# A decoder layer on one core: score shift on GpSimd, value sums in PSUM, scan factor in k's bank, tokens added by an accumulating DMA

## The reference

```python
x = x + rwkv(layernorm(x))          # time mix with a scan over tokens, then its own ffn
x = x + xattn(layernorm(x), ctx, ctx)
x = x + ffn(layernorm(x), U1, V1, b1, U2, V2, b2)

# in rwkv: h = ln1(x); xk, xv, xr = mixes of h and the h of the token before
k, v, sr = xk @ Wk.T, xv @ Wv.T, sigmoid(xr @ Wr.T)
y, (aa, bb, pp) = scan over tokens:  y = (e1*aa + e2*v) / (e1*bb + e2), with running maximum pp
x = x + (sr * y) @ Wo.T
h = ln2(x); kk = square(relu(xk @ Wkey.T)); x = x + sigmoid(xr @ Wrec.T) * (kk @ Wval.T)

# xattn: inside each token, 16 heads of 16; head i attends to heads 0..i of the same token's ctx
scores = einsum('bsqd,bskd->bsqk', qh, kh) / 4 ; masked below the diagonal; softmax
out    = einsum('bsqk,bskd->bsqd', attn, vh)

# ffn: low rank, 256 -> 64 -> 1024 -> gelu -> 64 -> 256
```

## Time and profile before

| | |
|---|---|
| Median of 3 runs | 1250.37 us (1248.64 to 1262.07) |
| Time of the profiled execution | 1249.77 us |
| Its span, first to last instruction | 1247.8 us |
| Mean granted TensorE clock | 0.945 |
| Busy: PE, DVE, ACT, POOL | 83%, 89%, 75%, 69% of the span |
| HBM | 29.38 MB read, 8.39 MB written |

### The profile page before, as it was taken

One profiled execution on the slowest core, in us unless ns is written; L12 is line 12 of the kernel. 1 busy time (PEld: TensorE's weight loads), 2 busy tenths in 40 slices (PEclk: granted clock), 3 DMA queues, 4 the chain that ended last, 5 costly groups with the idle time before them and its releaser, 6 DMA issues.

```text
span 1247.8 us, 14567 instructions
## 1 busy us (share of the span) xinstructions
PE 1032.6 (83%) x3584; PEld 584.6 (47%) x3584; DVE 1111.0 (89%) x2172; ACT 935.8 (75%) x2005; POOL 867.1 (69%) x783
## 2 busy tenths in 40 slices
PE   2679598989898989989798989989698998869515
PEld 1336263636455463736355463736346363626202
DVE  3755999999999999999999999999999999988681
ACT  4877779698888889796788879697688979464413
POOL 0112968788795968687595968688496968777680
PEclk9789799999999999999899999999899999979657
DMA  5010101001010101010010102001010101010000
GB/s 186 17 51 18 34 1 34 18 18 51 17 51 18 51 17 50 0 48 20 17 50 18 51 0 68 0 18 50 17 50 17 34 1 51 1 34 18 1 17 17
DMA packets 38964, 38.39 MB, mean 31 GB/s; under 512 B 2932, under 2 KB 38648, under 8 KB 38904
## 3 DMA queue, kind: packets, MB, share of 16 engines
q1 hardware_dynamic: 38904, 37.77, 9.5%
HBM read 29.38 MB, written 8.39 MB: 30 GB/s over the span
## 4 chain that ended last, share of the span: by engine, by line
PE 44%; DVE 32%; ACT 11%; issue 7%; POOL 4%; SPq 1%; DMA 0%; DVEq 0%; ACTq 0%; POOLq 0%
PE bank L813 19%; PE bank L870 8%; DVE x L1364 6%; PE bank L901 5%; DVE stat L1154 4%; PE bank L820 4%; PE bank L894 3%; DVE aa L1265 3%; PE bank L913 2%; DVE pp L1222 2%; POOL prod L338 2%; PE bank L885 2%; POOL prod L350 2%; DVE x L1306 2%; ACT n L462 2%
## 5 line engine op out<-in xcount | busy, mean ns | idle before, releaser
L338 POOL TENSOR_TENSOR prod<-q,kv_ctx 128x256 f32<-128x256 f32 (+5 forms) x448 | 394.7, 920 | 221.1 <-ACT q L462 221.1
L350 POOL TENSOR_TENSOR prod<-prob,v_dh 128x256 f32<-128x256 f32 (+3 forms) x256 | 390.9, 1568 | 29.2 <-ACT prob L564 29.2
L813 PE MATMUL bank<-xk,w_key 128*128 128x512 f32 x512 | 241.8, 612 | 17.6 <-DVE xk L1196 17.6
L870 PE MATMUL bank<-w_val,hidden 128*128 128x256 f32 x1024 | 225.9, 379 | 0.0
L870 PEld LDWEIGHTS bank<-w_val,hidden 128*128 128x128 f32 x1024 | 193.6, 190 | 32.4 <-issue 7.7
L1364 DVE TENSOR_REDUCE x<-prod 128x64 f32<-128x256 f32 (+3 forms) x256 | 189.9, 808 | 5.5 <-POOL prod L350 5.5
L1326 DVE TENSOR_REDUCE score<-prod 128x16 f32<-128x256 f32 (+5 forms) x448 | 175.5, 463 | 10.0 <-POOL prod L338 10.0
L813 PEld LDWEIGHTS bank<-xk,w_key 128*128 128x128 f32 x512 | 94.5, 194 | 141.8 <-issue 127.4
L548 ACT ACTIVATE hidden<-bank 128x512 f32<-128x512 f32 x128 | 74.9, 585 | 66.8 <-PE bank L813 66.7
L827 PE MATMUL bank<-ident,n 128*128 128x128 f32 x384 | 61.7, 297 | 75.5 <-ACT n L462 75.5
L422 ACT ACTIVATE lnv<-mv,eps_col 128x4 f32<-128x4 f32 x64 | 18.4, 287 | 127.2 <-DVE mv L1161 127.2
(11 more groups left out here) (96 smaller groups left out, 1946.4 us busy)
## 6 DMA issues: line engine op xcount, KB each, us to landing
x_in<-in_x SPq DMA_DIRECT2D x16, 512.0 KB, 3.6
kv_ctx<-in_ctx SPq DMA_DIRECT2D x16, 512.0 KB, 3.7
n<-in_x SPq DMA_DIRECT2D x16, 512.0 KB, 3.5
out<-y_out SPq DMA_DIRECT2D x16, 512.0 KB, 4.5
w_key<-in_wkey SPq DMA_DIRECT2D x1, 1024.0 KB
w_val<-in_wval SPq DMA_DIRECT2D x1, 1024.0 KB
w_k<-in_wk SPq DMA_DIRECT2D x1, 256.0 KB, 3.8
w_v<-in_wv SPq DMA_DIRECT2D x1, 256.0 KB, 4.2
```

The costliest lines, as they stand in the source:

```text
L338: ins = pool.tensor_tensor(o, a, b, ALU.mult)
L350: ins = pool.tensor_tensor(o, ph[:, HB * n:HB * n + HB, 0:keys].unsqueeze(2).to_broadcast(shape), vh[:, :, 0:keys].unsqueeze(1).to_broadca ...
L813: mm = pe.matmul(to[:, :], w[:, fi, P * f:P * f + P], src[:, fi, :], start=(fi == 0), stop=(fi == CH - 1))
L870: mm = pe.matmul(bank[6 + t // 2][:, C * (t % 2):C * (t % 2) + C], hidden[:, j, P * t:P * t + P], w_val[:, j, :], start=(j == 0), stop=(j ...
```

## The change

- **Score shift**: `shift_scores` goes from DVE to POOL. It is the same instruction, 128x512, twice a group. `sum_scores` now also waits for the shift of the group before.
- **Value sums and their division**: `sum_values` writes into PSUM bank 5 instead of `x3`, `over_mass` works in that bank, and `third_residual` reads it. One bank serves both halves, so the sums of the second half wait for the residual of the first. `project_rec` and `transpose_4` share bank 4 for both halves.
- **Scan factor**: e1 is no longer a tile in SBUF. `split_rise` and `exp_e1` write it to k's bank f, and the scans of aa and bb read it there. `project_r`, which overwrites the bank, waits for `aa_done` instead of `rise_done`.
- **Tokens**: the second load of x and `add_x_again` go. POOL issues a DMA that adds x from HBM to x1 in SBUF (`accum_op`), once a group, and `second_residual` waits for it.
- **Small**: `ln_den` takes `scale=2.0` and `inverse_den` loses its bias; the context is loaded two passes later; the vectors are loaded before the first tokens.
- **Orders**: the `step` of every engine is laid anew, and the loop's cut lies elsewhere, so that stages appear under other `on(n)`.

```diff
         def _(sp):
+            sp.dma_start(vec[:, :], vecs).then_inc(vec_loaded, 16)
             sp.dma_start(x_in[:, :, :], x_g[0]).then_inc(x_loaded, 16)
-            sp.dma_start(vec[:, :], vecs).then_inc(vec_loaded, 16)
...
                 if some(g - 1):
-                    sp.wait_ge(v_dh_done, upto(g - 2, 1))
-                    sp.wait_ge(s_prod, upto(g - 2, 4))
+                    sp.wait_ge(v_prod, upto(g - 2, 4))
                 sp.dma_start(kv_ctx[par][:, :, :], ctx_g[g]).then_inc(ctx_loaded, 16)
-
-            def load_x_again(g, par):
-                sp.wait_ge(x1_done, upto(g, 2))
-                sp.dma_start(n1[par][:, :, :], x_g[g]).then_inc(x_again, 16)
...
+            def shift_scores(g, s):
+                rows = slice(2 * NH * s, 2 * NH * s + 2 * NH)
+                pool.wait_ge(top_done, upto(g, 2, s + 1))
+                if some(g):
+                    pool.wait_ge(v_prod, upto(g - 1, 4, 2 * s + 2))
+                pool.tensor_tensor(prob[:, rows, :], score[:, rows, :],
+                                   top[:, rows].unsqueeze(2).to_broadcast([P, 2 * NH, NH]), ALU.subtract)\
+                    .then_inc(shift_done, 1)
...
+            def add_x(g, par):
+
+                pool.wait_ge(n2_done, upto(g, 1))
+                pool.wait_ge(stats_read[2], upto(g, 2))
+                if some(g):
+                    pool.wait_ge(x_added, 16 * g)
+                pool.dma_start(x1[par][:, :, :], x_g[g], accum_op=ALU.add).then_inc(x_added, 16)
...
                 act.wait_ge(rise_done, upto(g, 2, f + 1))
-                act.activation(e1[:, f, :], rr[:, f, :], ACT.Relu)
+                act.activation(bank[f][:, :], rr[:, f, :], ACT.Relu)
...
-                act.activation(e1[:, f, :], e1[:, f, :], ACT.Exp, scale=-1.0).then_inc(e1_exp, 1)
+                act.activation(bank[f][:, :], bank[f][:, :], ACT.Exp, scale=-1.0).then_inc(e1_exp, 1)
...
-                act.activation(rr[:, f, :], rr[:, f, :], ACT.Ln).then_inc(den_ln, 1)
+                act.activation(rr[:, f, :], rr[:, f, :], ACT.Ln, scale=2.0).then_inc(den_ln, 1)
...
-            token_major(bank[4 + s], s, xr, w_rec, rec_mm)
+            token_major(bank[4], s, xr, w_rec, rec_mm)
...
-            transposes(bank[4 + f], f, n4, tr4_mm)
+            transposes(bank[4], f, n4, tr4_mm)
...
-                    pe.wait_ge(rise_done, upto(i - 1, 2, 1))
+                    pe.wait_ge(aa_done, upto(i - 1, 2, 1))
                     project_r(i - 1, 0)
                 if on(1):
-                    pe.wait_ge(rise_done, upto(i - 1, 2))
+                    pe.wait_ge(aa_done, upto(i - 1, 2))
                     project_r(i - 1, 1)
...
-                    ins = dve.tensor_tensor_scan(bb[:, SEQ * f + s, 1:T + 1], e1[:, f, cols],
+                    ins = dve.tensor_tensor_scan(bb[:, SEQ * f + s, 1:T + 1], bank[f][:, cols],
                                                  e2[:, f, cols], 0.0, ALU.mult, ALU.add)
...
-                dve.wait_ge(res_done, upto(g, 1))
+                dve.wait_ge(x_added, 16 * (g + 1))
                 dve.scalar_tensor_tensor(out=pair(x2[par], s), in0=bank[6 + s][:, :], scalar=0.5,
                                          in1=pair(x1[par], s), op0=ALU.mult, op1=ALU.add).then_inc(x2_done, 1)
...
-            def sum_values(g, par, t, slot):
+            def sum_values(g, t, slot):
                 dve.wait_ge(v_prod, upto(g, 4, t + 1))
-                if t == 0 and some(g - 1):
-                    dve.wait_ge(y_done, upto(g - 2, 2))
+                if t == 0 and some(g):
+                    dve.wait_ge(x3_done, upto(g - 1, 2))
+                if t == 2:
+                    dve.wait_ge(x3_done, upto(g, 2, 1))
...
+                    row = C * (t % 2) + HB * HD * n
+                    ins = dve.tensor_reduce(bank[5][:, row:row + HB * HD], src, AX.X, ALU.add)
...
-                dve.tensor_tensor(pair(x3[par], s), pair(x3[par], s), pair(x2[par], s), ALU.add).then_inc(x3_done, 1)
+                dve.tensor_tensor(pair(x3[par], s), bank[5][:, :], pair(x2[par], s), ALU.add).then_inc(x3_done, 1)
```

More of the change, by code:

```diff
@@ L400, in _ @@
+                if on(3):
+                    add_x(i - 3, 1 - p)
+                if on(4):
+                    pool.wait_ge(v_sum, upto(i - 4, 4, 1))
+                    value_products(i - 4, 3, 1)
             drive(pool, step, step, step)
@@ L1385, in step @@
             def step(i, p, on):
-                if on(2):
+                if on(4):
+                    sum_values(i - 4, 1, 2)
+                    inverse_mass(i - 4, 0)
+                    over_mass(i - 4, 0)
+                    third_residual(i - 4, p, 0)
+                    stats_4(i - 4, p, 0)
+                    inverse_mass(i - 4, 1)
+                if on(2):
+                    divide_num(i - 2, 0)
+                if on(4):
+                    sum_values(i - 4, 2, 0)
+                if on(1):
+                    att_before_k(i - 1, 0)
+                    att_before_v(i - 1, 0)
+                    att_before_k(i - 1, 1)
+                if on(3):
+                    gate_values(i - 3, 0)
+                if on(1):
+                    att_before_v(i - 1, 1)
+                if on(3):
+                    second_residual(i - 3, 1 - p, 0)
+                if on(1):
+                    att_before_r(i - 1, 0)
+                if on(4):
+                    sum_values(i - 4, 3, 1)
+                if on(1):
+                    scan_pp(i - 1, 0)
+                    rise(i - 1, 0)
+                if on(3):
+                    stats_3(i - 3, 1 - p, 0)
+                    gate_values(i - 3, 1)
+                    second_residual(i - 3, 1 - p, 1)
+                    stats_3(i - 3, 1 - p, 1)
+                    mean_3(i - 3)
+                if on(2):
+                    divide_num(i - 2, 1)
+                if on(4):
+                    over_mass(i - 4, 1)
+                if on(1):
+                    scan_pp(i - 1, 1)
+                if on(4):
+                    third_residual(i - 4, p, 1)
+                if on(1):
+                    rise(i - 1, 1)
+                if on(4):
+                    stats_4(i - 4, p, 1)
+                    mean_4(i - 4)
+                if on(2):
+                    first_residual(i - 2, p, 0)
+                if on(1):
+                    att_before_r(i - 1, 1)
+                    scan_bb(i - 1, 0)
+                    weigh_token(i - 1, 0)
+                if on(2):
+                    first_residual(i - 2, p, 1)
+                    stats_2(i - 2, p, 0)
                     stats_2(i - 2, p, 1)
+                if on(1):
+                    scan_aa(i - 1, 0)
+                if on(2):
                     mean_2(i - 2)
@@ L1390, in step @@
                     weigh_token(i - 1, 1)
-                    scan_aa(i - 1, 0)
+                    scan_bb(i - 1, 1)
                     scan_aa(i - 1, 1)
@@ L1456, in step @@
-                if on(1):
-                    divide_num(i - 1, 0)
-                if on(2):
-                    gate_values(i - 2, 1)
-                    second_residual(i - 2, p, 1)
-                    stats_3(i - 2, p, 1)
-                    mean_3(i - 2)
-                if on(1):
-                    divide_num(i - 1, 1)
-                if on(0):
-                    scan_pp(i, 0)
-                if on(3):
-                    over_mass(i - 3, 1 - p, 1)
-                if on(0):
-                    rise(i, 0)
@@ L1471, in step @@
-                if on(3):
-                    third_residual(i - 3, 1 - p, 1)
-                    stats_4(i - 3, 1 - p, 0)
-                if on(0):
-                    scan_pp(i, 1)
-                    att_before_v(i, 1)
-                    rise(i, 1)
-                if on(3):
-                    stats_4(i - 3, 1 - p, 1)
-                    mean_4(i - 3)
-                if on(1):
-                    first_residual(i - 1, 1 - p, 0)
-                    first_residual(i - 1, 1 - p, 1)
```

508 lines of the change are left out of this document (223 added, 285 removed).

## The result

| | before | after |
|---|---|---|
| Median on the same chip | 1251.55 us (4 runs, 1248.64 to 1262.07) | 1301.28 us (4 runs, 1300.32 to 1302.38) |
| Ratio, 95% interval | | 1.0499 [1.0429, 1.0569] |
| Profiled execution, its span | 1249.77, 1247.8 | 1302.38, 1300.7 |
| Granted clock, mean | 0.945 | 0.933 |

The change makes the kernel 5% slower. The prediction said 1208 and gave slower a chance of 0.08.

What follows compares the result with a forecast made beforehand. The prediction took DVE, busy 89%, as the bound, other engines close behind. From 1249.8 us, 13 groups of 67.5 instead of 910.3 in all give -32.8, the end -9, the head 0: 1208 us, range 1160 to 1246.

Steps and rivals of the forecast that it cites:

- the wait of divide_num in its new place: First half's division inside the value products on DVE: can be held, but sum_values(2) behind it waits for them anyway; nothing added.
- rival D: Contention moves to divide_num, held 5.9 us more at one in sixteen: about 10 us, 1218; chance 0.06 for costs above 10.
- the prediction's own price of 5.9 us: Extra wait of one held divide_num, through the accumulating DMA's issue and the last value products on POOL.
- the walk: One steady group followed through the new orders of all engines: 67.5 us, 13 groups -32.8 us; chance 0.50 for 66 to 69.
- the head: The part ahead of the 13 steady groups: change 0, with +-4 us for latency of loads and single groups.
- the end: The part behind the steady groups: long waits on the path go, 3 us is given back, -9 us.
- DVE's terms: DVE's savings per group from shift, second token addition, scans and division by the mass: busy time 66.8 to about 60 us.
- POOL's: POOL's work per group: two shifts 2.4 us and DMA issue 1.0 added, contention time regained; 54.6 to 54.7 us.
- the chain: DVE from mean_3 to the aa scans, project_r's new wait for them, PE to val(3), back to mean_3: 67.5 us a group.
- A: Ties resolve well and PE is the only bound: 64.5 us a group, 1169 us; chance 0.20.
- B: POOL's return path over q becomes the bound: 69.5 us a group, 1234 us; chance 0.14.
- C: The accumulating DMA lands late and holds second_residual on DVE: up to 72.3 us a group, 1270 us; chance 0.10.

Runs made afterwards that it cites:

- e1: The changed kernel with the first half's divide_num moved on DVE from ahead of sum_values(2) to behind sum_values(3): 1219.24 us, ratio to before 0.9784.
- e5: The changed kernel with divide_num moved, the scan factor back in SBUF, and project_r waiting for the rise only instead of aa: 1277.76 us, ratio 1.0394.
- b2: The kernel before, unchanged, profiled once more: 1232.73 us in one run.
- e1b: The changed kernel with the first half's divide_num behind sum_values(3), run again beside the kernel before: 1218.55 us, ratio 0.9868.
- e4: The changed kernel with divide_num moved and the scan factor back in SBUF, project_r still waiting for aa: 1279.21 us, ratio 1.0411.
- the series: Three series of 60, 60 and 84 trials, not the kernel: DVE issues one instruction (two scans in eight trials) within a POOL queue; no kernel time.
- e6: The changed kernel with divide_num moved and the score shift back on DVE, behind top_scores: 1255.87 us, ratio 1.0179.

## Why the prediction was wrong

**The step that failed is the wait of divide_num in its new place, which the sum put at nothing and rival D at 10 us.** It took some 80 us over the 13 groups (961.8 in all, 882.1 in e1). Two statements carried it. "The instruction behind it, sum_values(2), must wait for that same product set anyway": it does not. In the trace after, the set is done at 468.83 and the division issued at 469.46, so nothing is hidden, and behind sum_values(2) stand the mixed rows of k, for which PE waits. And "at one in sixteen, as now": it was 14 in 14. The rate was an average over other instructions at other places, five long ones of 80, and nothing in the trace said that it would keep at this one. By the prediction's own price of 5.9 us, 13 holds give 77 us over the walk, 1285; that was never put down as a rival. In fact a hold cost 6.95 us of DVE's time and 6.1 of the group's.

**The walk was right to 11 us.** It said 67.5 us a group, and e1, which differs from the change by the place of one instruction, has 68.0 (67.9 with the first). In spans against the earlier trace rows: the 13 groups -28.2 where -32.8 was forecast, the head +2.7 where 0, the end -5.7 where -9; together -31.2 for -42. Three small misses on one side, 11 us.

**DVE's terms were right.** 60.36 us of its time a group in e1 (241.43 in a window of 272, four groups), where 60 was said; scans 0.67, division by the mass 0.70, value sums unchanged. POOL's too: the shift 1.07 (1.19 was said), the DMA's issue 1.0 to 1.1 (1.0), together 53.6 + 1.1 a group in e1 where 54.7 was said.

**The reason given for the chain was not.** e5 takes away the wait of r for aa, and the kernel takes as long as with it. The scans themselves are on the path, not the bank.

**The rivals.** A (PE alone, 64.5) and B (no idle time of POOL for q) didn't occur: POOL is idle for q 20.3 us after and 14.0 in e1, where 6 to 10 was said, so its chain is looser than the prediction held. (The 11 us of before stand in the earlier trace rows; the earlier trace rows has ACT's path to q.) C, to which nearly all of "slower" went, is refuted: the DMA lands in 5.4 us, where 7 was taken and 6.5 was covered. Its upper price, 11.3, was read from a wait that ended 20 us into the kernel before (the next longest, 9.4, at 89), and says nothing of a steady group. The right sign had its chance on the wrong mechanism.

**What the change is worth.** Against a before with two holds (b2) or its median on that chip, e1b gains 14 to 18 us, 1.3%. Where neither is held, the change as e1b has it takes a group from 68.8 to 67.9 us. By e4 the scan factor alone is worth 4.1 in these orders, so the rest of the change may cost some 3 (an estimate: no run takes it apart). The further lead over the first measurement of before, 1251.55, goes with holds, of which e1 and e1b show none. e1 beats both kernels, and it is the version to keep.

## What to carry to other kernels

When DVE and POOL both work on SBUF, list each DVE instruction with two SBUF inputs and look at what POOL has queued at its place. A place inside a run of POOL instructions may cost the whole rest of the run, in each turn of the loop (here up to 8.74 us for an instruction of 0.66); move the instruction to where POOL waits, or give it one operand in PSUM. When an accident happens once in sixteen in a trace, price its happening every time before trusting the rate, and give that price a line among the rivals.

## What the runs showed of the hardware

- A DVE instruction with two SBUF inputs, issued while POOL is busy, waits in one of two ways: for the POOL instruction in flight (all of the series, most of e6), or until POOL has nothing left to run (5.99 to 12.97 us). Every long hold in these traces ended 0.5 to 1.1 us after POOL's last queued instruction, with POOL waiting for something else. By the Trainium skill ("SBUF — State Buffer", section "Summary: rules for kernel authors") the second one to issue is blocked until the first finishes; that covers only the first way.
- The choice isn't set by the moment of issue: 0.8 us into the same product gave 2.13 and 7.95 us.
- A queue of POOL's that contains a DMA issue (1.07 us) holds DVE across it as well (469.46 to 477.44).
- The kernel before spreads over 26 us in 13 runs on one chip; e1, whose divide_num always runs while POOL idles, over 2 in 4 runs. That the holds make the spread is argued from the profiles, not shown.
- A 512 KB DMA that adds to its destination in SBUF lands 5.4 us after issue (median), plain loads of the same size 3.4 and 4.6 in the same trace (medians for x_in and for the context).
